# Turning the expert rows by DMA transposes of 16-bit halves instead of on TensorE, from the ninth tile of each layer on

## What is computed

```python
def _L0_ffn_ref(x, Wg, Wu, Wd, W1, W2):
    probs = jax.nn.softmax(xt @ Wg, axis=-1)
    topv, topi = jax.lax.top_k(probs, TOP_K)
    topv = topv / jnp.sum(topv, axis=-1, keepdims=True)
    h = _gelu(jnp.einsum('td,edf->tef', xt, Wu))      # F = 512
    y = jnp.einsum('tef,efd->ted', h, Wd)
    moe = jnp.einsum('ted,te->td', y, cw)
    ...
def _L1_ffn_ref(x, router_w, router_b, w1, b1, w2, b2):
    ...
    def body(i, acc):
        h = jax.nn.gelu(xf @ w1[i] + b1[i], approximate=False)   # F = 1024
        out_i = h @ w2[i] + b2[i]
        gate_i = jnp.sum(gates * (sel == i), axis=-1, keepdims=True)
        return acc + out_i * gate_i
```

## Time and profile before

| | us |
|---|---|
| median of 3 runs | 1671.32 |
| lowest and highest | 1669.58, 1675.81 |
| span of the profiled execution | 1669.4 |
| TensorE busy in the span | 1569.7 (94%) |
| VectorE busy | 823.6 (49%) |
| ScalarE busy | 734.2 (44%) |
| POOL busy | 714.7 (43%) |

### The profile page before, as it was taken

How to read it: one execution, slowest core, us unless ns; L and a number is a source line. 1 busy time by engine, 2 the same in 40 slices (tenths; PEclk the granted TensorE clock), 3 DMA queues, 4 the chain that set the end, 5 groups by cost and what they waited for, 6 DMA issues and landing times.

```text
span 1669.4 us, 32480 instructions
## 1 busy us (share of the span) xinstructions
PE 1569.7 (94%) x11054; PEld 1210.1 (72%) x11054; DVE 823.6 (49%) x2298; ACT 734.2 (44%) x1923; POOL 714.7 (43%) x815
## 2 busy tenths in 40 slices
PE   6989989999999999999997799988999999999997
PEld 3545445555548999998664567768999999999996
DVE  6867898787812223221477788873221122222220
ACT  4544545555541222222566466644333233333332
POOL 3122336666523555553810467752333333333332
PEclk9989999999999999999999999999999999999999
DMA  8534325534305222222621396466222222222221
GB/s 269 131 103 110 79 70 105 106 91 103 67 17 230 73 70 72 72 70 88 216 103 65 102 221 99 78 123 259 33 38 39 33 39 39 34 37 39 34 38 23
DMA packets 86093, 151.07 MB, mean 90 GB/s; under 512 B 16276, under 2 KB 64272, under 8 KB 82864
## 3 DMA queue, kind: packets, MB, share of 16 engines
q1 hardware_dynamic: 61392, 111.62, 25.3%
q0 software_dynamic: 24544, 37.38, 10.3%
HBM read 104.10 MB, written 44.45 MB: 89 GB/s over the span
## 4 chain that ended last, share of the span: by engine, by line
PE 79%; DVE 9%; DMA 4%; issue 3%; ACT 3%; SPq 1%; POOL 0%; another core or an unknown queue 0%; DVEq 0%; ACTq 0%; POOLq 0%
PE PS L1634 23%; PE PS L1652 22%; PE PS L1491 4%; PE PS L1427 3%; DVE PS L1954 3%; PE PS L1741 3%; PE PS L1476 3%; PE PS L1455 2%; PE PS L1608 2%; PE PS L1562 2%; PE PS L1619 2%; PE PS L1517 2%; PE PS L1437 2%; PE PS L1753 1%; DMA arena<-FD 1%
## 5 line engine op out<-in xcount | busy, mean ns | idle before, releaser
L1634 PEld LDWEIGHTS PS<-arena 128*128 128x128 f32 x3408 | 396.6, 192 | 15.8 <-DVE arena L2174 4.6
L1634 PE MATMUL PS<-arena 128*128 128x128 f32 x3408 | 403.8, 275 | 3.2 <-DVE arena L2174 3.2
L1652 PE MATMUL PS<-arena 128*128 x1704 | 392.4, 379 | 0.0
L1652 PEld LDWEIGHTS PS<-arena 128*128 128x128 f32 x1704 | 311.7, 190 | 40.2 <-issue 0.2
L2174 DVE COPY arena<-PS 128x256 f32<-128x256 f32 x142 | 60.3, 425 | 414.8 <-PE PS L1619 404.2
L1954 DVE CUSTOM_DVE_ANT_0 PS<-PS,arena 128x512 f32<-128x512 f32 (+3 forms) x512 | 235.5, 523 | 46.1 <-PE PS L1455 42.4
L970 POOL DMA_INDIRECT out<-arena x71 | 111.8, 1574 | 313.1 <-ACT arena L1246 292.4
L1236 ACT ACTIVATE arena<-PS,arena 128x128 f32<-128x128 f32 x568 | 162.3, 369 | 137.6 <-PE PS L1634 137.5
L1246 ACT ACTIVATE arena<-PS,arena 128x256 f32<-128x256 f32 x142 | 67.4, 474 | 283.1 <-PE PS L1654 191.3
L903 POOL TENSOR_SCALAR_AFFINE_SELECT arena<-arena 128x256 f32<-128x256 f32 x256 | 100.0, 414 | 207.9 <-ACT arena L1152 207.5
L1152 ACT ACTIVATE arena<-PS 128x512 f32<-128x512 f32 (+1 forms) x256 | 166.3, 704 | 49.9 <-PE PS L1476 40.3
(11 more groups left out here) (246 smaller groups left out, 1985.6 us busy)
## 6 DMA issues: line engine op xcount, KB each, us to landing
arena<-FD SPq DMA_DIRECT2D x32, 512.0 KB
arena<-in_w SPq DMA_DIRECT2D x16, 1024.0 KB
SPL<-arena SPq DMA_DIRECT2D x32, 384.0 KB, 2.6
arena<-SPL SPq DMA_DIRECT2D x64, 192.0 KB
XN<-arena SPq DMA_DIRECT2D x16, 512.0 KB, 3.2
arena<-SPL SPq DMA_DIRECT2D x64, 128.0 KB
arena<-SUM SPq DMA_DIRECT2D x16, 512.0 KB, 6.4
arena<-in_x SPq DMA_DIRECT2D x8, 512.0 KB, 6.4
```

The lines of the kernel that those rows point to most:

```text
L1634: ins = pe.matmul(o, m.now[i % 2][:, c * F + 128 * f:c * F + 128 * f + 128], m.xt[i % 2][:, 128 * c:128 * c + 128], start=(c == 0), stop=( ...
L1652: ins = pe.matmul(to, m.hT[i % len(m.hT)][:, 128 * c:128 * c + 128], m.WD[:, bass.ds(e * (nf * 256) + c * 256, 256)], start=(c == 0), stop ...
```

## The change

Tiles 0 to 7 of each layer are turned as before. From tile 8 on (`TURNED` = 8; 63 tiles in each layer) a tile goes another way:

1. `halve` on VectorE reads the gathered fp32 rows as pairs of 16-bit numbers and writes all low halves of a row, then all high halves, into `halves[i % 2]` (128x512 of 16 bits). It stands last in VectorE's iteration, four tiles ahead.
2. `rows_across` on SP issues one DMA transpose of that buffer into `across[i % 2]`, as four 128x128 blocks.
3. VectorE's `tile_turn` puts the halves of each number together again, from `across` into `xt[i % 2]`, in the place in which it copied from PSUM.

A gather now waits for the tile that had its buffer to be halved (or turned, for tiles under 8), and POOL issues the gathers one tile earlier, five ahead. The other edits only let several semaphores be shared (`pads_set`, `const_set`, `b_cut`).

```diff
@@ row_read, new
+        def row_read(layer, i):
+            if i < TURNED:
+                return x_turned, TURNED * layer + i + 1
+            return x_halved, (NTILE - TURNED) * layer + i - TURNED + 1
@@ sync, behind layer 0's weight loads, and at the very end for layer 1
+            def rows_across(layer):
+                for i in range(TURNED, NTILE):
+                    m = MOE[layer]
+                    sp.wait_ge(x_halved, (NTILE - TURNED) * layer + i - TURNED + 1)
+                    if i >= TURNED + 2:
+                        sp.wait_ge(xt_put, NTILE * layer + i - 1)
+                    sp.dma_start_transpose(m.across[i % 2].rearrange("p (k n) -> p k n", k=4), m.halves[i % 2]).then_inc(x_across[i % 2], 16)
+            rows_across(0)
...
+            rows_across(1)
@@ gpsimd, gather and experts
                 if i >= 4:
-                    pool.wait_ge(x_turned, NTILE * layer + i - 3)
+                    pool.wait_ge(*row_read(layer, i - 4))
...
             def experts(layer):
+                gather(layer, 4)
                 for i in range(NTILE):
-                    gather(layer, i + 4)
+                    gather(layer, i + 5)
@@ tensor, tile_turn
-                if i >= NTILE:
+                if i >= TURNED:
                     return
@@ vector, tile_turn
-                dve.wait_ge(x_turned, NTILE * layer + i + 1)
                 if i >= 2:
                     dve.wait_ge(up_made, (i - 1, NTILE + 2 * (i - 1))[layer])
-                dve.tensor_copy(m.xt[i % 2][:, :], ps(0, o, o + 256)).then_inc(xt_put)
+                if i < TURNED:
+                    dve.wait_ge(x_turned, TURNED * layer + i + 1)
+                    dve.tensor_copy(m.xt[i % 2][:, :], ps(0, o, o + 256)).then_inc(xt_put)
+                    return
+                uses = (NTILE - TURNED + 1 - i % 2) // 2
+                dve.wait_ge(x_across[i % 2], 16 * (layer * uses + (i - TURNED) // 2 + 1))
+                dve.tensor_copy(m.xt[i % 2].bitcast(U16).rearrange("p (n k) -> p k n", k=2), m.across[i % 2].rearrange("p (k n) -> p k n", k=2)).then_inc(xt_put)
@@ vector, halve, new, and its place in the loop
+            def halve(layer, i):
+                if not TURNED <= i < NTILE:
+                    return
+                m = MOE[layer]
+                dve.wait_ge(tile_in[i % 4], 16 * (layer * ((NTILE + 3 - i % 4) // 4) + i // 4 + 1))
+                if i >= TURNED + 2:
+                    dve.wait_ge(x_across[i % 2], 16 * (layer * ((NTILE - TURNED + 1 - i % 2) // 2) + (i - TURNED) // 2))
+                dve.tensor_copy(m.halves[i % 2].rearrange("p (k n) -> p k n", k=2), m.xr[i % 4].bitcast(U16).rearrange("p (n k) -> p k n", k=2)).then_inc(x_halved)
...
                 for i in range(NTILE):
                     weights(layer, i + 2)
                     tile_turn(layer, i + 2)
+                    halve(layer, i + 4)
```

More of the change, by code:

```diff
@@ L10 @@
 U32 = mybir.dt.uint32
+U16 = mybir.dt.uint16
 ALU = mybir.AluOpType
@@ L33 @@
 LAG1 = 6
+TURNED = 8
 SLOTS = [((0, 0, 3), (3, 0, 2), (5, 0, 1)), ((0, 0, 3), (3, 1, 2), (5, 2, 1))]
@@ L516, in experts_room @@
             if layer == 0:
+                top[0] = (base + 8192 + 7) // 8 * 8
+                r.halves, r.across = ([view(carve(256), 256, U16) for _ in range(2)] for _ in range(2))
+                assert top[0] <= hs_at
                 top[0] = moe0_at
@@ L528, in experts_room @@
             if layer:
+                top[0] = (top[0] + 7) // 8 * 8
+                r.halves, r.across = ([view(carve(256), 256, U16) for _ in range(2)] for _ in range(2))
                 assert top[0] <= NT * D + 2 * T
@@ L564, in build @@
         logitT = sem("logitT")
-        stk_set, v_set = sem("stk_set"), sem("v_set")
+        pads_set = sem("pads_set")
         qk_made, hi_cut, mid_cut, lo_cut = sem("qk_made"), sem("hi_cut"), sem("mid_cut"), sem("lo_cut")
@@ L576, in build @@
         zero0, zero1 = sem("zero_xs0"), sem("zero_rest")
-        b_in, b_cut, b_rows, b_set = sem("b_in"), sem("b_cut"), sem("b_rows"), sem("b_set")
+        b_in, b_cut, b_rows = sem("b_in"), sem("b_cut"), sem("b_rows")
         b1_turned, b1_put = sem("b1_turned"), sem("b1_put")
@@ L587, in build @@
         r_pos = sem("r_pos")
-        none_set, slot_in, slot_turned, slot_off, slot_put = (sem(n) for n in ("none_set", "slot_in", "slot_turned", "slot_off", "slot_put"))
+        slot_in, slot_turned, slot_off, slot_put = (sem(n) for n in ("slot_in", "slot_turned", "slot_off", "slot_put"))
         row_out = [sem(f"row_out{n}") for n in range(4)]
@@ L594, in build @@
         x_turned = sem("x_turned")
+        x_halved = sem("x_halved")
+        x_across = [sem(f"x_across{n}") for n in range(2)]
         xt_put = sem("xt_put")
@@ L699, in maxrow @@
                 sp.wait_ge(s_made, 24 * n + 24)
-                sp.wait_ge(stk_set, 3)
+                sp.wait_ge(pads_set, 7)
                 if n >= 3:
@@ L711, in clear @@
                 sp.wait_ge(cst_in, 32)
-                sp.wait_ge(none_set, 4)
+                sp.wait_ge(const_set, 7)
                 if p == 0:
@@ L752, in sync @@
                     slots(0)
-            sp.wait_ge(b_cut, 5)
-            sp.wait_ge(b_set, 1)
+            sp.wait_ge(b_cut, 6)
             for k in range(3):
@@ L880, in gpsimd @@
             for v in Vb:
-                pool.memset(v, 0.0).then_inc(v_set)
-            pool.wait_ge(v_set, 2)
+                pool.memset(v, 0.0).then_inc(pads_set)
+            pool.wait_ge(pads_set, 2)
             for v in Vb:
-                pool.memset(v[:, :, :, 16:17], 1.0).then_inc(v_set)
-            pool.wait_ge(v_set, 4)
+                pool.memset(v[:, :, :, 16:17], 1.0).then_inc(pads_set)
+            pool.wait_ge(pads_set, 4)
             for n in range(3):
                 if n:
-                    pool.wait_ge(stk_set, n)
-                pool.memset(STK[n][1][96:99, :, :].rearrange("p j s -> p (j s)").bitcast(F32), ONES2).then_inc(stk_set)
-            pool.wait_ge(stk_set, 3)
+                    pool.wait_ge(pads_set, 4 + n)
+                pool.memset(STK[n][1][96:99, :, :].rearrange("p j s -> p (j s)").bitcast(F32), ONES2).then_inc(pads_set)
+            pool.wait_ge(pads_set, 7)
             def clear_meta():
                 for n, apart in enumerate((128, 0)):
[L894 to L897, removed]
+                    pool.memset(unused[n][0:NTILE, :, :], 0.0).then_inc(const_set)
+                    pool.wait_ge(const_set, 2 * n + 4)
+                    pool.iota(unused[n][0:NTILE, :, 1], [[1, 128]], base=T, channel_multiplier=apart, allow_small_or_imprecise_dtypes=True).then_inc(const_set)
+                pool.wait_ge(const_set, 7)
             def future(h):
@@ L909, in bias_rows @@
             def bias_rows():
-                pool.memset(B2S, 0.0).then_inc(b_set)
+                pool.memset(B2S, 0.0).then_inc(b_cut)
                 pool.wait_ge(b_in, 32)
@@ L913, in bias_rows @@
                     if k:
-                        pool.wait_ge(b_cut, 2 * k)
+                        pool.wait_ge(b_cut, 2 * k + 1)
                     pool.tensor_copy(b3[0:8, k, :], bstage[0:8, :]).then_inc(b_cut)
                     if k < 2:
-                        pool.wait_ge(b_cut, 2 * k + 1)
+                        pool.wait_ge(b_cut, 2 * k + 2)
                         pool.tensor_tensor(bstage[0:8, :], bstage[0:8, :], b3[0:8, k, :], ALU.subtract).then_inc(b_cut)
@@ L1129, in project_v @@
                 act.wait_ge(v_made, 2 * b + half + 1)
-                act.wait_ge(v_set, 4)
+                act.wait_ge(pads_set, 4)
                 if b >= 2:
```

## The result

The changed kernel takes 1642.66 us (median of 4 runs, 1638.89 to 1650.07), the kernel before 1670.64 (4 runs). The medians are 28.0 us apart, 1.7%; the ratio of the runs is 0.9824 with a 95% interval of 0.9802 to 0.9846, so the kernel is faster beyond the scatter. The forecast was 1643.6.

The account below looks back on a forecast made before the run. TensorE was taken as the bound, busy 94% of the span and every microsecond of the expert stages. Removing 27.7 us from the profiled 1669.4 gives 1641.7; adding 1.9 to reach the median gives 1643.6, range 1637 to 1677.

Parts of the forecast that it names:

- What it removes: Expert stages: 63 tiles x 2 layers x 0.22 us of TensorE, 27.7 us; tiles then take 3.52 and 7.16 us.
- VectorE: Added merge and split at 0.69 us each make its iteration 3.03 us in layer 0, 4.2 in layer 1; hidden under TensorE.
- the 0.86: Layer 0, VectorE: us counted from gelu's end to the start of the weights copy, including loading the expert's number.
- rival 2: VectorE becomes layer 0's bound, deciding from 0.94 us a copy; with copies of 1.23 us, +9 us, 1680; chance 0.06.
- The gather's wait: Layer 0: the split waits 0.3 to 1.2 us for its gather to land; nothing reaches TensorE.
- The transpose: SP's DMA transpose takes 3.5 us from split to merge, bounds 2.0 to 7.7, and fits under 5.5 in layer 0.
- L: Time from the end of a split to the start of its merge, taken as 3.5 us.
- within 4 us: Sign that the forecast is right: in the middle of each stage a transpose lands in that time.
- The ring: Split, transpose, merge, split every two tiles; binds if split-to-merge time exceeds 5.5 us in layer 0, 12.8 in layer 1.
- Layer 1's start: Transposes queue on SP behind 8 MB of down weights, which are through before the first merge; cost nothing.
- Rival 1: Layer 0's transpose is late and the kernel slower: at the upper bound, 7.7 us, +40 us, about 1711; chance 0.16.
- rival 4: No gain: transposes, gathers and adding DMAs contend on the DMA engines and `y` buffers free late; 1671; chance 0.07.

Follow-up runs that it names:

- the run with pairs: The changed kernel with every DMA transpose made twice, the second waiting for the first to land: 1702.09 us in one run.
- one tile ahead: The changed kernel with each tile split three tiles ahead instead of four, leaving its transpose one VectorE iteration instead of two: 1650.22 us in one run.
- the repeat: The changed kernel unaltered, run again beside a faster version on the same chip: 1648.59 us (5 runs), ratio to before 0.9841.

## Why the prediction was right, step by step

- **What it removes**: right. 63 x 0.22 us per layer; tile times 3.52 and 7.15 to 7.16. Taking the 0.22 from the distance of starts and not the 0.38 of the row was the decisive reading: 126 x 0.38 would have said 48 us. Restoring the two transposes took the whole gain back. In the profiles 2.2 us of the 27.7 are missing from the stages, nearly all at their starts, and 1.7 came from outside them: that the sum met the forecast this closely is chance.
- **VectorE**: right that it is hidden, too high in size at both terms. The copies are 0.43 and 0.45 us against the 0.69 taken (the lower bound was the truth: the step of two numbers did not keep a 16-bit copy at the 0.686 of the plain row), and the 0.86 is a latency and only in part work. The iteration is near 2.0 us, not 3.03. The turning point of rival 2 was therefore put too low: with copies made three times, 1.5 us for the merges and 1.4 for the splits against its 0.94 a side, layer 0 only just falls back to the old 3.74.
- **The gather's wait**: right on the mean, 0.96 us against 0.3 to 1.2, too low at the top (2.1), and harmless: with no split and no merge the stages take the same time.
- **The transpose**: right in that it is hidden; L is 2.70 in the middle, 3.25 in the run with pairs, against 3.5, but "within 4 us" does not hold for the rare long ones, up to 4.94 and once 5.3. The ring itself was seen closing in one run only (one tile ahead); the run meant to close the ring of two tiles ran into SP's queue first, so its turning point of 5.5 us was not seen. The two statements of the Trainium skill can now be told apart for this shape: "VectorE: DVE Perf Modes" (The three transpose paths), 1309 ns per 128x128 block, would have made four blocks an estimated 5.2 us; one transpose of all four takes 2.7 with its issue. Its advice (Rules for kernel authors) to turn on TensorE where PSUM will do is wrong for this kernel, in which TensorE is the bound and the DMA latency is hidden two iterations deep. "Advanced Engine Details and Errata" (X-Bar Transpose), as fast as plain DMAs, holds roughly for the latency (a 384 KB store lands in 2.6, a 128 KB load in 2.0) but not for the load, below.
- **Layer 1's start**: right, with about 1 us between the last of the weights and the first transpose; starting four tiles earlier cost 10 us.
- **The rivals**: none came. Rival 1's mechanism is real, as the run with one tile ahead shows, for a ring of one tile; rival 4's contention did not reach the time although the DMA share doubled.
- **The base**: the forecast compares with a median whose runs scatter by some 10 us, as the repeat (1648.6) shows. That it came within 1 us of the first median is partly luck; the 27 us of difference is not.

## What to carry to other kernels

Where one engine is busy all the time, price a removed instruction by the distance between the starts of its neighbours and not by its own row, and move it to an idle path even if it takes ten times longer there, as long as the ring of buffers has time: by the working above, latency plus copies, divided by the number of tiles in flight, has to stay under one tile time. Ask of the new path what stands ahead of it in its queue: here a start four tiles earlier, behind 8 MB of loads, gave back 10 of the 27 us. To measure a latency that is hidden, take one buffer's worth of lead away; chaining the operation twice measured the issuing queue instead.

## What the runs showed of the hardware

- A DMA transpose within SBUF of 128x512 16-bit numbers into four 128x128 blocks took 2.5 us at the least and 2.70 in the middle from the end of the copy that feeds it to the start of the copy that reads it, with 4.94 as the longest, in the run with one tile ahead; with two per tile, one behind the other, 3.25 us in the middle from issue to landing. SP spends 1.19 us of this on the issue, and up to 2.5 now and then; behind 8 MB of loads in its queue 4.83 and 11.01.
- It loads the DMA engines more than its bytes say. The queue that carries it in layer 0, 545 to 765 us of the changed kernel (packets, MB, share of 16 engines):

```profile
q1 hardware_dynamic: 33391, 8.05, 19.2%
```

  It adds (154639 - 86093) / 126 = 544 packets each, 240 bytes on the mean, so these are 61 transposes, and 0.192 x 16 x 220 = 676 engine-us for them are 11.0 each, for 0.13 MB. The gather and the storing DMA of a tile together take 12.3 (21.8% of the same stretch, 62.5 tiles) and move twice that. Layer 1's share, 0.32 over 7.15 us against 0.22 over 7.37, gives about the same, 10.7.
- Copies of 16-bit numbers within SBUF whose one side steps by two numbers took 0.43 and 0.45 us for 128x512, the same as the conversion with both sides dense (0.427).
